# Backward sums of a two-layer GNN kernel: groups of four supertiles with shared node blocks

## The chip, the cores and the metric

The kernel runs on one core of a Trainium2 chip. A time is the device time of one execution in microseconds (us), and where several runs are told of, their median. Engines are named as in the profile: PE is TensorE's matmul, PEld its weight load, DVE is VectorE, ACT is ScalarE, POOL is GpSimd, SP is SyncE. Full speed of TensorE's clock is 2.4 GHz, its lower level is 1.2 GHz; the profile gives the granted clock as a share of full speed.

## What is computed

Two graph layers on 3125 nodes of 256 features and 100000 edges. The second one, whose backward half is changed here, is this (cut; `_typed_pass` is called once along the edges and once against them):

```python
def _typed_pass(feat, W, bias, src_idx, dst_idx, etypes, norm_per_edge, n):
    proj = jnp.einsum('ni,rio->rno', feat, W)          # 16 relations, 256 x 256 each
    m = proj[etypes, src_idx] + bias
    m = m * norm_per_edge[:, None]
    return segment_sum(m, dst_idx, num_segments=n)
norm_f = _inv_degree(dst, n)[dst]
m_forward = _typed_pass(feat, Wf, forward_bias, src, dst, etypes, norm_f, n)
norm_b = _inv_degree(src, n)[src]
m_backward = _typed_pass(feat, Wb, backward_bias, dst, src, etypes, norm_b, n)
s = feat @ loop_weight
return s + s + self_bias + m_forward + m_backward
```

The backward pass takes for each edge the row `proj[type, dst]` and adds it to the sum of node `src`; the sum is divided by the node's degree at the end.

## The kernel before

Edges are handled in 196 supertiles of 512 edges (128 partitions x `J` = 4). The nodes are 25 blocks of 128. `acc` in SBUF holds for each block 256 sums and, in two more columns (`AW` = 258), the degree.

The kernel has three long stages on the same engines: the first layer's messages, the forward sums (beside which the backward projections are computed and written to `proj[1]`), and last the backward sums, which alone are changed. Before the last stage the edges have been sorted by source node, not exactly: each supertile holds sources out of a few neighbouring blocks. `windows(1)` works out for each supertile the lowest block `lo`, the highest `hi` and a running count, and packs them in one word of `win[1]`; every engine reads these words with `windows_of`, a load followed by register arithmetic.

In the backward stage each engine runs its own loop, and semaphores alone order them:

- **POOL** (`sixes`, L431 to L442 by the profile's lines) gathers: for supertile `s` four indirect DMAs of 128 rows of 1 KB from `proj[1]` to slot `s % 12` of `raw2` (`RS` = 12). From supertile 12 on it waits before each supertile until `s_agg[2]` says that the supertile ten before it has been multiplied.
- **ACT** (`next_rows2`) copies the row numbers of later gathers into `gslot2`, two supertiles at a time.
- **DVE** (`compare2`, `add2`, driven by `backward`) makes one-hot keys of 128 x 1024 for each supertile (`match_nodes` at L1023: two blocks wide, for `lo` and `lo + 1`), in a ring of six (`HS`), four supertiles ahead; and adds the product, 2 x 258 columns in PSUM, to `acc` (L1081). If the supertile reaches beyond `lo + 1`, each further block is a round trip: keys of 128 x 512, a product in the PSUM bank `further_sums`, an addition (L1089).
- **PE** (`sum_backward`) waits for the keys, the gathered rows and the addition three supertiles back, then makes 8 f32 products of 128 x 258 (L745), 4 for each of two blocks, into one of three pairs of PSUM banks (`pair_sums`: `pu`, `pg`, `pa`). A further block is 4 more into `pc`, each after waiting for DVE. An f32 product stands in the profile as two LDWEIGHTS and two MATMUL, so that a supertile is 16 MATMUL there.

The bookkeeping of one supertile on PE and the waits in front of it are these lines:

```python
pe.wait_ge(s_oh[2], s + 1)
pe.wait_ge(s_gath[2][n], 16 * J * (rnd + 1))
if past(s, 3):
    pe.wait_ge(s_add[2], s - 2)
```

At the end `backward_mean` divides, and SP stores the result.

Of the kernel before, what the change touches and what calls it, by code (L numbers as in the profile page):

```python
# [4 lines left out]
F32 = mybir.dt.float32  # L5
F32R = mybir.dt.float32r
I32 = mybir.dt.int32
ALU = mybir.AluOpType
# [4 lines left out]
P = 128  # L13
# [5 lines left out]
J = 4  # L19
# [21 lines left out]
GS = 4  # L41
QS = 24
RS = 12
HS = 6
# [3 lines left out]
assert (ST - GS) % RS == 0  # L48


def gnn_program(nc, x, dst_l, src_l, typ_l, ea_t, W1, b1, W2, b2, Wg, bg, gamma, beta,
# [9 lines left out]
    with ctx:  # L61
# [88 lines left out]
        onehot2 = [fa[:, c:c + 2 * SE].rearrange("p (j n) -> p j n", j=J) for c in (8192, 9216, 4224, 5248, 2064, 3096)]  # L150
        further_onehot = fa[:, 6272:6272 + SE].rearrange("p (j n) -> p j n", j=J)
        PARTS = ((1, 0), (0, 1), (0, 0))

        pu = pb("pu", [P, HK, SE])
        pg = pb("pg", [P, J, H])
        pc = pb("pc", [P, J, H])
        pa = pb("pa", [P, 2, SE])
# [3 lines left out]
        pair_sums = [pu[:, :, :], pg[:, :, :].rearrange("p (a j) f -> p a (j f)", a=2), pa[:, :, :]]  # L161
# [140 lines left out]
        def sixes(eng):  # L302

            for s in range(RS + GS):
                yield s, s % RS, s // RS
            with eng.Fori(1, (ST - GS) // RS) as i:
                for m in range(RS):
                    yield RS * i + GS + m, (GS + m) % RS, i + (GS + m) // RS
# [80 lines left out]
        def _(pool):  # L389
# [226 lines left out]
        def _(pe):  # L616
# [122 lines left out]
            def sum_backward(s, n, rnd, w):  # L739

                lo, hi, wx = w

                def products2(out, keys):
                    for j in range(J):
                        last = nc.tensor.matmul(out[:, 0:AW], keys[:, j, :], raw2[:, n, j, :], start=(j == 0), stop=(j == J - 1))  # L745
# [9 lines left out]
                with pe.If(hi > lo + 1):  # L755
                    with pe.Fori(lo + 2, hi + 1) as b:
                        pe.wait_ge(s_xadd[2], wx + b)
                        pe.wait_ge(s_xoh[2], wx + b)
                        products2(further_sums, further_onehot).then_inc(s_xagg[2], 1)
# [81 lines left out]
            pe.wait_ge(s_add[1], ST)  # L841
            pe.wait_ge(s_win[1], 1)
            pe.wait_ge(s_ones, 1)
            for n, w in enumerate(windows_of(pe, 1, 0, GS)):
                sum_backward(n, n, 0, w)
            with pe.Fori(0, (ST - GS) // RS) as i:
                for m, w in enumerate(windows_of(pe, 1, RS * i + GS, RS)):
                    sum_backward(RS * i + GS + m, (GS + m) % RS, i + (GS + m) // RS, w)
# [3 lines left out]
        def _(dve):  # L852
# [45 lines left out]
            def windows(k):  # L898
# [3 lines left out]
                if k == 1:  # L902
                    link(nc.vector.tensor_scalar(first_neg, first_neg, float(2 - NB), None, ALU.max))
                    link(nc.vector.tensor_scalar(extra, first_neg, -1.0, 1.0, ALU.mult, ALU.add))
                    link(nc.vector.tensor_tensor(last, last, extra, ALU.max))
                link(nc.vector.scalar_tensor_tensor(out=extra, in0=last, scalar=float(-k), in1=first_neg, op0=ALU.add, op1=ALU.add))
                link(nc.vector.tensor_tensor_scan(count, extra, extra, float(NB), ALU.add, ALU.bypass))
                link(nc.vector.tensor_tensor(count, count, extra, ALU.subtract))
                link(nc.vector.scalar_tensor_tensor(out=count, in0=count, scalar=float(-k), in1=first_neg, op0=ALU.add, op1=ALU.add))
# [155 lines left out]
            def compare2(s, n, w):  # L1065

                lo, hi, wx = w
                if past(s, HS):
                    dve.wait_ge(s_agg[2], s - HS + 1)
                match_nodes(onehot2[n], iota_p, lo, s, src_f).then_inc(s_oh[2], 1)  # L1070

            def add2(s, n, w):

                lo, hi, wx = w
                first = dve.snap(nc.s_assert_within(lo, 0, NB - 2, skip_runtime_bounds_check_because="the windows are kept two blocks wide"))
                dve.wait_ge(s_xadd[2], wx + lo + 2)
                if past(s, 1):
                    dve.wait_ge(s_add[2], s)
                dve.wait_ge(s_agg[2], s + 1)
                t = acc[:, bass.ds(first, 2), :]  # L1080
                nc.vector.tensor_tensor(t, t, pair_sums[n % 3][:, :, 0:AW], ALU.add).then_inc(s_add[2], 1)  # L1081
                with dve.If(hi > lo + 1):
                    with dve.Fori(lo + 2, hi + 1) as b:
# [280 lines left out]
            for n, w2 in enumerate(windows_of(dve, 1, 0, 2)):  # L1364
                compare2(n, n, w2)
# [74 lines left out]
```

## Time and profile before

| | us |
|---|---|
| median of 3 runs | 4423.52 (4414.99 to 4432.65) |
| the profiled execution, own time | 4418.46 |
| its span, first to last instruction | 4416.7 |
| first to last gather issued in the backward stage | 3183.6 to 4367.5 |
| PE's first and last backward product | 3208.0 to 4397.9 |
| PE, DVE, POOL busy over the whole span | 79%, 56%, 52% |
| mean granted TensorE clock | 0.891 |

Matmuls are pipelined: two that follow each other start 0.22 us apart at full clock, while each is shown as 0.38 us long. So in the rows below 16 matmuls without a gap are shown as 3.65 us, and the next 16 begin 3.49 us after the first did. A number in square brackets in a timeline is the time that the engine had been idle, and what ended it; "issue" is a wait that the profile can't explain by a semaphore, "remote" one whose end the profile puts down to no engine or queue that it knows of.

### The profile page before, as it was taken

How to read it: one execution, taken by the hardware profiler on the slowest of the kernel's cores; microseconds unless marked ns; L12 is line 12 of the kernel's file. 1: busy time of each engine (PE TensorE's matmuls, PEld its weight loads, DVE VectorE, ACT ScalarE, POOL GpSimd, SP SyncE). 2: the span in 40 equal slices, each digit the busy share in tenths (PEclk: the TensorE clock that was granted, in tenths of full speed). 3: DMA queues.
4: the chain of work that ended last, by engine and by line, in shares of the span. 5: the costliest groups of instructions: out<-in, count | busy, mean ns of one | idle time of the engine just before them, and what ended most of it. 6: DMA issues, size and time to landing. Idle time of an engine off the chain costs nothing.

```text
span 4416.7 us, 72963 instructions
## 1 busy us (share of the span) xinstructions
PE 3478.9 (79%) x21136; PEld 2939.8 (67%) x21137; DVE 2476.3 (56%) x3465; ACT 1007.0 (23%) x1734; POOL 2308.7 (52%) x2362
## 2 busy tenths in 40 slices
PE   6999999999999979976666676767657766777776
PEld 5888888888888858864554555555445555665555
DVE  6888887888788888854554532222323333333334
ACT  3444444444444444410110110010100000000000
POOL 1555555555555500036555666656566655666663
PEclk8999999999999989988888888888867878888878
DMA  4555555555555525544443464444333322233332
GB/s 165 157 159 155 157 156 152 157 155 159 149 152 154 157 81 205 204 131 124 132 129 118 132 141 134 126 129 132 111 92 87 89 82 80 85 89 88 90 88 79
DMA packets 322746, 569.91 MB, mean 129 GB/s; under 512 B 73897, under 2 KB 218393, under 8 KB 322585
## 3 DMA queue, kind: packets, MB, share of 16 engines
q0 software_dynamic: 137984, 411.19, 33.2%
q1 hardware_dynamic: 182732, 154.33, 10.6%
q10 hardware_dynamic: 1868, 2.52, 0.2%
q8 instruction: 67, 1.10, 0.1%
q14 instruction: 95, 0.77, 0.1%
HBM read 452.43 MB, written 115.41 MB: 129 GB/s over the span
## 4 chain that ended last, share of the span: by engine, by line
PE 52%; issue 17%; DVE 12%; another core or an unknown queue 12%; DVEq 6%; ACT 1%; ACTq 0%; DMA 0%; POOL 0%; SPq 0%; POOLq 0%
PE pc L697 13%; PE pa L706 11%; PE pu L687 4%; PE pu L745 4%; PE pg L671 4%; PE pa L745 4%; PE pg L745 4%; DVE key L1249 3%; DVE tops L1246 3%; PE pu L679 3%; DVEq L277 1%; PE pu L800 1%; PE pc L659 1%; DVE onehot L1023 1%
## 5 line engine op out<-in xcount | busy, mean ns | idle before, releaser
L428 POOL DMA_INDIRECT fa<-proj,gslot x784 | 744.8, 950 | 865.6 <-issue 569.8
L416 POOL DMA_INDIRECT fa<-ptab,slot x784 | 814.2, 1039 | 721.8 <-issue 375.1
L440 POOL DMA_INDIRECT hr<-proj,gslot x784 | 745.8, 951 | 446.7 <-issue 226.3
L706 PE MATMUL pa<-fa,onehot 128*128 128x258 f32 x1760 | 517.1, 446 | 363.0 <-DVE onehot L1023 196.5
L706 PEld LDWEIGHTS pa<-fa,onehot 128*128 128x128 f32 x1760 | 379.7, 222 | 480.1 <-issue 374.8
L697 PE MATMUL pc<-ws,hr 128*128 128x256 f32 x4704 | 649.2, 290 | 43.2 <-issue 40.5
L697 PEld LDWEIGHTS pc<-ws,hr 128*128 128x128 f32 x4704 | 598.3, 193 | 64.5 <-issue 61.7
L745 PE MATMUL pu<-hr,fa 128*128 128x258 f32 x1056 | 295.6, 425 | 132.6 <-issue 129.2
L1056 DVE TENSOR_TENSOR acc<-acc,pa 128x258 f32 x196 | 82.7, 422 | 503.4 <-remote 303.8
L745 PEld LDWEIGHTS pu<-hr,fa 128*128 128x128 f32 x1056 | 225.2, 214 | 194.2 <-issue 157.5
L745 PE MATMUL pg<-hr,fa 128*128 128x258 f32 x1040 | 278.8, 417 | 74.5 <-issue 72.0
L1023 DVE SCALAR_TENSOR_TENSOR fa<-pc,base,src_f 128x1024 f32<-128x1024 f32 (+1 forms) x210 | 261.5, 1247 | 123.7 <-issue 109.3
L745 PE MATMUL pa<-hr,fa 128*128 128x258 f32 x1040 | 272.3, 408 | 67.2 <-issue 65.6
L503 ACT ACTIVATE hr<-pu 128x512 fp32r<-128x512 f32 x392 | 213.0, 596 | 459.5 <-remote 249.9
L745 PEld LDWEIGHTS pg<-hr,fa 128*128 128x128 f32 x1040 | 218.2, 211 | 129.0 <-issue 84.8
L1007 DVE SCALAR_TENSOR_TENSOR hr<-pu,hr 128x1024 fp32r<-128x1024 f32 x196 | 239.5, 1222 | 103.7 <-ACT hr L503 99.5
L745 PEld LDWEIGHTS pa<-hr,fa 128*128 128x128 f32 x1040 | 211.6, 204 | 115.3 <-issue 80.0
L514 ACT CAST hr<-fa 128x1024 fp32r<-128x1024 f32 x196 | 206.1, 1052 | 336.7 <-DVE fa L1030 293.6
L706 PE MATMUL pa<-hr 128*128 128x256 f32 x1760 | 251.4, 285 | 19.0 <-issue 13.8
L593 ACT COPY gslot<-row_dst 128x8 int32 (+1 forms) x98 | 18.8, 197 | 1083.9 <-DMA hr<-proj,gslot 1083.9
L1030 DVE TENSOR_TENSOR fa<-fa,pc 128x1024 f32<-128x1024 f32 x196 | 238.0, 1214 | 47.9 <-PE pc L697 29.5
L800 PE MATMUL pu<-hr 128*128 128x512 f32 x960 | 255.2, 409 | 8.5 <-issue 7.0
(153 smaller groups left out, 5048.8 us busy)
## 6 DMA issues: line engine op xcount, KB each, us to landing
proj<-fa SPq DMA_DIRECT2D x400, 256.0 KB
fa<-in_ea_t SPq DMA_DIRECT2D x196, 128.0 KB
fa<-ptab,slot POOLq DMA_INDIRECT x784
fa<-proj,gslot POOLq DMA_INDIRECT x784
hr<-proj,gslot POOLq DMA_INDIRECT x784
fa<-in_Wrel SPq DMA_DIRECT2D x32, 256.0 KB
ptab<-fa SPq DMA_DIRECT2D x25, 256.0 KB, 2.0
out<-res SPq DMA_DIRECT2D x4, 768.0 KB
```

Source lines behind the costliest of these rows:

```text
L416: pool.indirect_dma_start(pbuf[:, n % 2, j, :], None, ptab[:, :], bass.IndirectOffsetOnAxis(ap=slot[:, n, j:j + 1], axis=0)).then_inc(s_ga ...
L428: pool.indirect_dma_start(gbuf[:, n, j, 0:H], None, proj[0][:, :], bass.IndirectOffsetOnAxis(ap=gslot[:, at, j:j + 1], axis=0)).then_inc(s ...
L440: pool.indirect_dma_start(raw2[:, n, j, 0:H], None, proj[1][:, :], bass.IndirectOffsetOnAxis(ap=gslot2[:, n, j:j + 1], axis=0)).then_inc(s ...
L503: last = nc.scalar.activation(uT[:, par, 0, h, :, :].rearrange("p k e -> p (k e)"), pu[:, h, :], ACT.Relu)
L514: nc.scalar.copy(msg[:, par, 0, :, :], gate[:, par, :, :]).then_inc(s_mhi, 1)
L697: last = nc.tensor.matmul(pc[:, j, :], uT[:, par, a, j // 2, kk, j % 2 * P:(j % 2 + 1) * P], w2s[:, c, kk, :], start=False, stop=(j == jj ...
L706: last = nc.tensor.matmul(pa[:, bank, 0:width], keys[:, at, j, :], rows[:, j, :], start=(n == 0), stop=(n == len(todo) - 1))
L745: last = nc.tensor.matmul(out[:, 0:AW], keys[:, j, :], raw2[:, n, j, :], start=(j == 0), stop=(j == J - 1))
L800: last = nc.tensor.matmul(pslots[n], hT[:, a, kk, b * P:(b + 1) * P], wsp[:, u, c, kk, :], start=(not d and m == 0 and kk == 0), stop=(m = ...
L1007: nc.vector.scalar_tensor_tensor(out=uT[:, par, 1, :, :, :].rearrange("p h k e -> p h (k e)"), in0=pu[:, :, :], scalar=0.0, in1=uT[:, par, ...
L1023: return nc.vector.scalar_tensor_tensor(out=out, in0=numbers.unsqueeze(1).to_broadcast([P, J, width]), scalar=base[:, bass.ds(b, 1)], in1= ...
L1030: nc.vector.tensor_tensor(gate[:, par, :, :], gate[:, par, :, :], pc[:, :, :], ALU.mult).then_inc(s_msg, 1)
```

## The change

The unit of the backward sums becomes a group of four supertiles (49 groups) in place of one supertile.

- All PSUM banks become one tensor `banks`; the backward sums use two sets of three banks (`quad_sums`). The four supertiles of a group share a window of three blocks (`UB`), `lo` to `lo + 2`, where `lo` is the lowest of the group. The first two blocks are multiplied for every supertile, the third only for those that reach it (`third2` holds its keys in memory that is free by then). Since the third bank may get no product at all, a matmul of zeros opens it and another closes it in every group.
- All products of a group add up in PSUM; `s_agg[2]`, the addition on DVE (128 x 774) and `s_add[2]` come once per group.
- Blocks beyond the third are a round trip for the whole group.
- The ring of gathered rows has 16 slots in place of 12, the ring of keys 8 in place of 6. POOL waits once per group, for the group four before it, and DVE makes the keys of a group after the addition of the group two before it.
- `windows(1)` works out the windows of groups. The first group's keys are all made ahead of the last forward addition.

The core of the diff:

```diff
-RS = 12
-HS = 6
+RS = 16
+HS = 8
+UB = 3
...
-        pair_sums = [pu[:, :, :], pg[:, :, :].rearrange("p (a j) f -> p a (j f)", a=2), pa[:, :, :]]
+        quad_sums = [banks[:, 0:UB, :], banks[:, UB:2 * UB, :]]
...
-            for s, n, rnd in sixes(pool):
-                if past(s, RS):
-                    pool.wait_ge(s_agg[2], s - RS + 2)
+            for s, n, rnd, q in sixteens(pool):
+                if q >= RS // GS if isinstance(q, int) else n % GS == 0:
+                    pool.wait_ge(s_agg[2], q - RS // GS + 1)
...
-                pe.wait_ge(s_oh[2], s + 1)
-                pe.wait_ge(s_gath[2][n], 16 * J * (rnd + 1))
-                if past(s, 3):
-                    pe.wait_ge(s_add[2], s - 2)
-                for c in range(2):
-                    last = products2(pair_sums[n % 3][:, c, :], onehot2[n % HS][:, :, c * P:(c + 1) * P])
+                if past(q, 2):
+                    pe.wait_ge(s_add[2], q - 1)
+                nc.tensor.matmul(sums[:, 2, 0:AW], zeros[:, 0:P], zeros, start=True, stop=False)
+                lo, wx, most = w[0][0], w[0][2], bounded(pe, w[1][2])
+                for m in range(GS):
+                    n, at = n0 + m, (n0 + m) % HS
+                    pe.wait_ge(s_oh[2], GS * q + m + 1)
+                    pe.wait_ge(s_gath[2][n], 16 * J * (rnd + 1))
+                    if m == GS - 1:
+                        with pe.If(most > lo + 2):
...
+                    with pe.If(w[m][1] > lo + 1):
+                        products2(sums[:, 2, :], third2[at], n, stop=False)
+                    if m == GS - 1:
+                        nc.tensor.matmul(sums[:, 2, 0:AW], zeros[:, 0:P], zeros, start=False, stop=True)
+                    for c in range(2):
+                        last = products2(sums[:, c, :], onehot2[at][:, :, c * P:(c + 1) * P], n, start=(m == 0), stop=(m == GS - 1))
                 last.then_inc(s_agg[2], 1)
...
+            def compare_quad(q, at, w):
+                lo = w[0][0]
+                for n in range(GS):
+                    with dve.If(w[n][1] > lo + 1):
+                        match_nodes(third2[at + n], iota_p[:, 0:P], bounded(dve, lo + 2), GS * q + n, src_f)
+                    match_nodes(onehot2[at + n], iota_p, lo, GS * q + n, src_f).then_inc(s_oh[2], 1)
...
+            def add2(q, at):
+
+                lo, hi, wx = windows_of(dve, 1, GS * q, 1)[0]
...
+                dve.wait_ge(s_agg[2], q + 1)
+                t = acc[:, bass.ds(first, UB), :]
+                nc.vector.tensor_tensor(t, t, quad_sums[at // GS][:, :, 0:AW], ALU.add).then_inc(s_add[2], 1)
...
+            further_quad(0, windows_of(dve, 1, 0, 2))
+            next_quad(1, GS)
+            with dve.Fori(0, ST // GS // 2 - 1) as i:
+                for u in range(2):
+                    add2(2 * i + u, GS * u)
+                    next_quad(2 * i + 2 + u, GS * u)
```

How PE's instructions stand in the backward loop, before: one supertile (8 products into `pu`, then the jump over the further block, whose loop and products into `pc` stand behind it).

```order
L749 ISA
L745 MATMUL pu<-hr,fa 128x258 x8
L755 REGISTER_ALU x4
L755 COMPARE_AND_BRANCH
L756 ISA
L756 UNCONDITIONAL_BRANCH
L756 ISA
L757 REGISTER_ALU x2
L745 MATMUL pc<-hr,fa 128x258 x4
L756 ISA
L756 COMPARE_AND_BRANCH
L755 UNCONDITIONAL_BRANCH
```

After: the start of a group. L754 is the matmul of zeros, L768 guards the third block, whose keys are in `onehot` here.

```order
L281 TENSOR_LOAD win
L753 REGISTER_ALU
L754 MATMUL banks<-fa 128x258
L758 ISA
L759 ISA
L768 REGISTER_ALU x4
L768 COMPARE_AND_BRANCH
L749 MATMUL banks<-hr,onehot 128x258 x4
L768 UNCONDITIONAL_BRANCH
L749 MATMUL banks<-hr,fa 128x258 x8
```

The 8 products of a supertile stay as they were. The load of the windows comes once per group instead of once per twelve supertiles, the guarded products now stand ahead of a supertile's own and don't wait for DVE a second time, and the zero matmul is new.

DVE in the backward loop, before: the keys of one supertile (L1023), then the addition of one (L1081), in turn.

```order
L1023 REGISTER_ALU
L1023 ISA
L1023 SCALAR_TENSOR_TENSOR fa<-pc,base,src_f 128x1024
L1076 REGISTER_ALU x3
L1076 ISA
L1081 ISA
L1081 TENSOR_TENSOR acc<-acc,pg 128x516
L1082 REGISTER_ALU x3
L1082 COMPARE_AND_BRANCH
```

After: the addition of a group (L1129), and behind it the keys of the group two ahead, shown up to the first supertile's third block.

```order
L281 TENSOR_LOAD win
L1129 REGISTER_ALU
L1129 ISA
L1129 TENSOR_TENSOR acc<-acc,banks 128x774
L281 ISA
L281 TENSOR_LOAD win
L1099 REGISTER_ALU x4
L1099 COMPARE_AND_BRANCH
L1054 ISA
L1054 SCALAR_TENSOR_TENSOR onehot<-banks,base,src_f 128x512
L1099 UNCONDITIONAL_BRANCH
L1054 ISA
```

Four key instructions now follow one addition, and all four stand behind the wait for the group two before.

## Rows read from the trace of the kernel before

**Rows 1.** Windows, L440: stretch, POOL busy (gathers), granted clock, DMA share, GB/s.
```profile
3422.10:3869.20 447.10, 272.29 (x289) 0.82 0.29 84
3869.20:4345.10 475.90, 302.49 (x321) 0.83 0.31 88
3279.10:4345.10 1066.00, 665.52 (x705) 0.82 0.30 87
...
4174.40:4198.10 23.70, 15.12 (x16) 0.79 0.30 89
```
**Rows 2.** Timeline around two pauses of POOL: start, duration, engine, line, idle before.
```profile
4169.63 0.95 POOL L440 DMA_INDIRECT hr<-proj,gslot  x1 [0.30 <-issue]
4174.48 0.94 POOL L440 DMA_INDIRECT hr<-proj,gslot  x1 [3.90 <-remote]
...
4183.63 3.65 PE L745 MATMUL pg<-hr,fa 128*128 128x258 f32 x16
...
4187.12 0.82 PE L745 MATMUL pa<-hr,fa 128*128 128x258 f32 x3
...
4192.99 0.59 PE L745 MATMUL pa<-hr,fa 128*128 128x258 f32 x1 [2.22 <-issue]
...
4197.25 3.76 PE L745 MATMUL pa<-hr,fa 128*128 128x258 f32 x9 [0.81 <-issue]
4197.47 0.69 DVE L1081 TENSOR_TENSOR acc<-acc,pu 128x516 f32 x1 [10.20 <-remote]
4198.16 0.94 POOL L440 DMA_INDIRECT hr<-proj,gslot  x1 [3.99 <-remote]
```
**Rows 3.** Windows, L745: stretch, PE busy (matmuls), PEld busy (loads), clock, DMA, GB/s.
```profile
4174.40:4187.90 13.50, 13.50 (x58) 11.22 (x56) 0.92 0.33 95
4187.90:4197.20 9.30, 2.40 (x5) 1.04 (x4) 0.62 0.29 87
4197.20:4211.40 14.20, 14.15 (x57) 11.80 (x57) 0.89 0.31 88
```
**Rows 4.** Waits from 3183 to 4417: who waited for whom, us, times, longest.
```profile
DVE acc L1081 <- remote: 513.9, 64, 27.6
...
POOL hr L440 <- remote: 168.2, 52, 7.4
...
PE pc L745 <- DVE fa L1023: 82.4, 14, 16.0
```
**Rows 5.** Line L1023, 3255 to 4345: duration in ns, min/median/max; DVEq is DVE's sequencer.
```profile
L1023 DVEq FUSED_REGOPS  x196: 3/99/1394, 3255.7 to 4342.7; - x196
```
**Rows 6.** Start of the stage: POOL's first pauses in the timeline; PE's windows on L745.
```profile
3247.09 0.95 POOL L440 DMA_INDIRECT hr<-proj,gslot  x1 [0.30 <-issue]
3255.39 0.94 POOL L440 DMA_INDIRECT hr<-proj,gslot  x1 [7.35 <-remote]
...
3279.14 0.95 POOL L440 DMA_INDIRECT hr<-proj,gslot  x1 [4.06 <-remote]
...
3208.00:3222.00 14.00, 13.29 (x46) 10.68 (x46) 0.79 0.36 105
3222.00:3253.00 31.00, 6.27 (x11) 3.35 (x12) 0.54 0.32 93
```
**Rows 7.** Tile pc from 3180 on: count, ns min/median/max, first and last start.
```profile
L745 PE MATMUL pc<-hr,fa x112: 378/636/772, 3485.5 to 4139.0; 128*128 128x258 f32 x112
```
**Rows 8.** Groups by form, 3550 to 4417: busy us, mean ns of one, idle before.
```profile
L1023 DVE SCALAR_TENSOR_TENSOR fa<-pc,base,src_f 128x1024 f32<-128x1024 f32 x141 | 180.8, 1282 | 84.8 <-issue 76.5 <-PE pg L745 4.7 <-PE pa L745 2.9
L1081 DVE TENSOR_TENSOR acc<-acc,pg 128x516 f32 x48 | 33.0, 687 | 120.1 <-remote 104.1 <-PE pg L745 9.8 <-PE pa L745 3.5
L1023 DVE SCALAR_TENSOR_TENSOR fa<-pc,base,src_f 128x512 f32<-128x512 f32 x11 | 8.2, 750 | 7.0 <-issue 7.0
L1089 DVE TENSOR_TENSOR acc<-acc,pc 128x258 f32 x12 | 5.1, 424 | 43.9 <-PE pc L745 26.9 <-remote 12.3 <-issue 4.7
```
**Rows 9.** Timeline of the stage's end.
```profile
4367.49 0.94 POOL L440 DMA_INDIRECT hr<-proj,gslot  x1 [0.30 <-issue]
...
4370.22 3.65 PE L745 MATMUL pa<-hr,fa 128*128 128x258 f32 x16
...
4394.63 3.65 PE L745 MATMUL pu<-hr,fa 128*128 128x258 f32 x16
...
4398.52 0.69 DVE L1081 TENSOR_TENSOR acc<-acc,pu 128x516 f32 x1 [2.80 <-PE pu L745]
```
**Rows 10.** DMA queues, whole span (page) and 3320 to 4360: packets, MB, share of 16 engines.
```profile
q8 instruction: 67, 1.10, 0.1%
...
q0 software_dynamic: 32944, 89.98, 30.0%
```

More of the change, by code:

```diff
@@ L737, in sum_projections, with sum_backward, products2 @@
                 sum_further(k, n % 2, [gbuf[:, n, :, :]], AW, w)
-            def sum_backward(s, n, rnd, w):
-                lo, hi, wx = w
-                def products2(out, keys):
+            def sum_backward(q, n0, rnd, w):
+                sums = quad_sums[n0 // GS % 2]
+                def products2(out, keys, n, start=False, stop=True):
                     for j in range(J):
-                        last = nc.tensor.matmul(out[:, 0:AW], keys[:, j, :], raw2[:, n, j, :], start=(j == 0), stop=(j == J - 1))
+                        last = nc.tensor.matmul(out[:, 0:AW], keys[:, j, :], raw2[:, n, j, :], start=(start and j == 0), stop=(stop and j == J - 1))
@@ L902, in windows @@
                 if k == 1:
[L903 to L907, printed above, removed]
@@ L908, in windows @@
-                link(nc.vector.tensor_tensor(count, count, extra, ALU.subtract))
-                link(nc.vector.scalar_tensor_tensor(out=count, in0=count, scalar=float(-k), in1=first_neg, op0=ALU.add, op1=ALU.add))
+                    quads_of = lambda t: t.rearrange("p (q n) -> p q n", n=GS)
+                    least, most, more, total = (extra[:, n * ST // GS:(n + 1) * ST // GS] for n in range(4))
+                    nc.vector.tensor_reduce(least, quads_of(first_neg), AX.X, ALU.max)
+                    link(nc.vector.tensor_reduce(most, quads_of(last), AX.X, ALU.max))
@@ L1063, in add_sums, with further_quad @@
                 dve.sem_inc(s_done, 1)
[L1065 to L1083, printed above, removed]
+            def compare_quad(q, at, w):
[4 more added lines that the diff above has]
+                    match_nodes(onehot2[at + n], iota_p, lo, GS * q + n, src_f).then_inc(s_oh[2], 1)
+            def further_quad(q, w):
+                lo, wx, most = w[0][0], w[0][2], bounded(dve, w[1][2])
+                with dve.If(most > lo + 2):
+                    with dve.Fori(lo + 3, most + 1) as b:
                         dve.wait_ge(s_xadd[2], wx + b)
-                        match_nodes(further_onehot, iota_p[:, 0:P], b, s, src_f).then_inc(s_xoh[2], 1)
-                        dve.wait_ge(s_add[2], s + 1)
+                        for n in range(GS):
+                            last = match_nodes(further_onehot[n], iota_p[:, 0:P], b, GS * q + n, src_f)
+                        last.then_inc(s_xoh[2], 1)
                         dve.wait_ge(s_xagg[2], wx + b)
@@ L1089, in add2, with next_quad @@
                         nc.vector.tensor_tensor(t, t, further_sums[:, 0:AW], ALU.add).then_inc(s_xadd[2], 1)
+                        dve.wait_ge(s_xadd[2], wx + b + 1)
+            def next_quad(q, at):
+                w = windows_of(dve, 1, GS * q, GS)
+                compare_quad(q, at, w)
+                further_quad(q, w)
+            def add2(q, at):
+                lo, hi, wx = windows_of(dve, 1, GS * q, 1)[0]
+                first = dve.snap(nc.s_assert_within(lo, 0, NB - UB, skip_runtime_bounds_check_because="the windows are kept three blocks wide"))
+                if past(q, 1):
+                    dve.wait_ge(s_add[2], q)
+                dve.wait_ge(s_agg[2], q + 1)
+                t = acc[:, bass.ds(first, UB), :]
+                nc.vector.tensor_tensor(t, t, quad_sums[at // GS][:, :, 0:AW], ALU.add).then_inc(s_add[2], 1)
             def add_first(s, par, w):
```

88 lines of the change are left out of this document (50 added, 38 removed).

## The prediction, made blind

> **What bounds the kernel now.** Only the last 1.2 ms can change, so I read that stage alone: first the windows of POOL's gathers, then the timeline around its pauses, then PE's windows, last who waited for whom. The stage ends when PE has multiplied the last supertile; some 20 us of division and store follow and stay. Its pace is very even. Supertiles 16 to 191 take 1066.0 us (705 gathers in the window, of which 704 are these), 24.2 us for four; in the later half 475.9 us for 80, 23.8 us for four [rows 1].
>
> No engine is full. Four supertiles are 16 gathers, which POOL issues 1.25 us apart: 19.7 us. Then it pauses for 4.0 us, and the next 16 begin 23.7 us after the first 16 did [rows 1, 2]. PE has 64 matmuls for four supertiles, 14.0 us at full clock (16 take 3.49 us). But it does not do them evenly: 58 in the first 13.5 us, 5 in the next 9.3 us, and 57 in the 14.2 us after that [rows 3]. In that slow stretch PE is idle before single matmuls of one supertile, where there is no semaphore to wait for, at 2.2 and 0.8 us each, "issue"; DVE's sequencer needs up to 1.39 us for a register operation that mostly takes 0.10 [rows 2, 5]; and an addition whose product PE had finished by 4187.3 starts only at 4197.47, "remote", as POOL's pause ends at 4198.16 [rows 2]. In sum DVE waits 513.9 us and POOL 168.2 us for "remote" [rows 4]. So something that comes with unbroken gathering slows PE's and DVE's sequencers and the semaphores between the engines, from some 10 to 14 us after a burst of gathers begins until some 3 us after it ends. At the start of the stage the same is larger: 48 gathers without a pause, and in the last 31 us of them PE does 11 matmuls, half clock included [rows 6]. I can't name the mechanism, but its shape is clear: **POOL's unbroken gathering is what stops PE, and POOL stops only when the ring is full.** PE's capacity in one such cycle is some 64 to 67 matmuls, just what four supertiles need.
>
> **The change, part by part.** Against the profiled execution (4418.5 us, 5 us under the median):
>
> (a) *Ring of 16.* The first burst grows from 48 gathers to 64, which is 16 x 1.25 = 20 us more of crawling. Then POOL waits for a whole group of PE's (68 matmuls and its third blocks), where it waited for two supertiles. Before, supertile 16 is gathered from 3279.1 on [rows 6]. After: first gather at 3183.6 as before, 64 gathers end by about 3268, slow stretch over by 3274 (it outlasted the first burst by 5 us). DVE makes 4 keys instead of 2 and some third blocks ahead of the last forward addition, 2 x 1.28 + 4 x 0.75 = 5.6 us [rows 8], so PE starts near 3214. It does some 25 matmuls at speed and 22 in the crawl (11 in 31 us), and the rest of the first group, some 50, at 0.22 to 0.43 us: 11 to 21 us, done near 3290. **+11 us**, bounds +5 and +20.
>
> (b) *Blocks beyond two.* They are 112 matmuls in 14 round trips [rows 7], where PE waited 82.4 us for DVE, 16.0 at most [rows 4]. I followed the kernel's sorting on the reference's edges: it gives these 14, and after the change 29 supertiles that reach a third block and no group that reaches a fourth. So all round trips go. What that is worth shows in the pace: 24.2 us for four supertiles against 23.7 in the regular cycle, over the 44 groups from supertile 16 on 1066.0 - 44 x 23.7 = **-23 us**; the waits were mostly time in which the cycle would have stood anyway.
>
> (c) *Third blocks.* 29 supertiles x 8 matmuls, of which 23 lie in those 44 groups (groups 10 to 36, 13 of them). One costs 8 x 0.22 = 1.75 us at full and 3.4 at half clock. Since PE's capacity per cycle is just used up, and POOL now waits for the end of the group, they come after the slow stretch and lengthen the pause: 23 x 2.0 = **+46 us**, bounds 0 (they fit in a slow stretch) and 78.
>
> (d) *Matmuls of zeros.* Two products, 4 matmuls of 258 columns, 0.9 us for each group: 64 become 68, and 44 x 0.9 = 39 us if all are on the path. Up to 67 matmuls fit into a cycle by the rows above, so I take **+9 us**, bounds 0 and 39.
>
> (e) *Hand-overs.* Additions on DVE: 196 of 0.69 us become 49 of about 0.95 (258 columns take 0.42, 516 take 0.69 [rows 8]), some 90 us of DVE's busy time, all of it beside PE. Key instructions stay at 1.28 us. DVE's sequencer has, counted in the order of instructions, some 95 operations for four supertiles before and some 65 after, PE's about the same. **0**: DVE makes the keys of a group behind the addition of the group two before, 1 + 1 + 4 x 1.28 = 7 to 10 us with loads, while PE is in the group between, 15 us or more. Its cover is gone when the slow stretch catches the last keys; that is a rival below. PE's and DVE's increments fall by 147 each. The Trainium skill, "TensorE: Matmul & The Clock Gate", section on the per-tile semaphore tail, says that increments serialize, at 26 ns each; by it the 147 of PE are worth 4 us and the sum would be 4 us lower. The trace has no row for that; what it shows of semaphores is the 10.20 us wait above.
>
> (f) *The end.* Before, PE ends at 4398.3 (4394.63 and 3.65) [rows 9], 53 us after the gathers of supertile 192 begin (4345.1). After, when the last group's gathers have ended (19.7 us) and the slow stretch is over (3 us), PE has three groups of 68 matmuls left, 14.8 us each at the pace of [rows 9], 45 with some at half clock: 68 us. **+15 us**, bounds +8 and +18.
>
> Sum: 11 - 23 + 46 + 9 + 0 + 15 = **+58 us**. From the median of 4423.5: 4481.5, say 4482. Bounds added up: 5 - 23 + 0 + 0 + 8 = -10 and 20 - 23 + 78 + 39 + 18 = +132. For the likeliest case by itself 4440 to 4550.
>
> **Rivals.**
> 1. *The extra matmuls are absorbed.* PE enters a cycle a little further on, the zeros and two thirds of the third blocks fall into the slow stretch, and the pause stays at 4 us, set by the delivery of the semaphore. For it: "PE finished, semaphore late" is what [rows 2] show, and the pauses are equal to 0.1 us. Sum 11 - 23 + 15 + 0 + 12 = +15: 4438, no change. Chance 0.18.
> 2. *Fewer hand-overs shorten the slow stretch.* If sequencer operations and increments share what the gathers crowd, a third fewer on DVE could let PE finish a group inside the burst, and the pause falls from 4.0 to 2.5: 44 x 1.5 = 66 us less, third blocks at 20: 11 - 23 - 66 + 20 + 13 = -45: 4378. Against it: the gathers keep their 1.25 us throughout and are by far the most of the traffic. Chance 0.15.
> 3. *POOL becomes the bound.* No pauses: 196 x 5.0 = 980 us from 3184 to 4168, the last group 15 us later, against 4398.3: about 215 us less, 4208. It decides if PE's 73 matmuls a group (16 us) go on beside gathering. The first burst [rows 6] speaks against it. Chance 0.08.
> 4. *DVE becomes late.* Four keys stand in a row after one wait, some 30 sequencer operations; if half fall where one takes 0.7 us or more, the last keys come after the slow stretch, and PE waits 2.5 us in each group: 44 x 2.5 = 110 on top, 4592. It decides where a fourth key comes later than 10.5 us (three supertiles) into PE's group. Chance 0.06.
> 5. *The loops are loaded anew in each round.* PE's loop grows to sixteen supertiles with third and further blocks, some 1,350 instructions. In the stage before no instruction packet is seen between 3320 and 4360, though the whole run has 67 of 16 KB on one queue [rows 10]. Their share (0.1% of 16 engines over 4416.7 us) makes one about 1.1 us; six in each of twelve rounds, all on the path, are +79: 4561. The Trainium skill, "Runtime: NRT & Kernel Launch", section Instruction fetch mechanics, says that a taken branch out of the resident instructions forces a load, and gives PE 2048 instructions; by that figure the loop would still fit and this rival costs nothing. Chance 0.03.
>
> **How the numbers follow.** The forecast has 0.50. A measurement of this kernel can tell 0.5% (22 us) from no change, so faster is below 4401, slower above 4446. Rivals 2 and 3 are faster; rival 1 and the low end of the forecast are the same; the rest is slower: 0.23, 0.18, 0.59. The range leaves out rival 3 and part of 2 below, rivals 4 and 5 above: 4350 to 4550, some 0.8 inside.
>
> **What would show it.** Right: POOL's bursts of 16 with pauses of 4 to 5 us, longer (6 to 10) in the middle of the stage; PE idle at "issue" within groups; first pause of POOL after 64 gathers, near 3268, lasting some 20 us; no wait of PE for keys above some us; last gather near 4400. Wrong in the base: pauses clearly under 4 us, or a slow stretch that begins later than 14 us into a burst (rivals 2, 3); third blocks without longer pauses (rival 1); PE waiting for DVE at the third or fourth supertile of a group (rival 4); instruction packets within the stage (rival 5).

## The result, and the profile of the changed kernel

The changed kernel takes 4461.14 us (median; 4459.14 to 4463.66), the kernel before 4420.71 us in the same measurement: ratio 1.0088, 95% interval 1.0065 to 1.0111. It is slower by 0.9%, some 40 us; 4482 was forecast. The profiled run took 4459.21 us, with a span of 4457.4 us and a mean granted clock of 0.896, so its trace can stand beside that of [rows 1 to 9].

One thing has to be said first, because half of the experiments can't be read without it: the kernel before takes 4414 to 4421 us on the chip of this measurement and on one of the chips used below, and 3765 us on three others; every comparison below is between kernels that ran on one chip, and says on which kind.

POOL's windows on its gathers (columns: stretch, POOL busy with the number of gathers, granted clock, DMA share, GB/s), changed kernel; they answer to [rows 1]. The stretches are supertiles 16 to 191, the first 64 gathers, and the time from supertile 192's first gather to PE's end:

```profile
3289.10:4371.10 1082.00, 665.49 (x704) 0.85 0.30 85
3186.40:3271.40 85.00, 65.78 (x64) 0.60 0.34 98
4371.10:4438.80 67.70, 15.12 (x16) 0.95 0.11 31
```

POOL's timeline in the changed kernel (start, duration, engine, line, operation, idle before it in brackets): the first pause of the stage, two regular ones, one behind a group with four third blocks, and the last four of the stage:

```profile
3270.43 0.95 POOL L444 DMA_INDIRECT hr<-proj,gslot  x1 [0.30 <-issue]
3289.12 0.94 POOL L444 DMA_INDIRECT hr<-proj,gslot  x1 [17.74 <-PE banks L749]
...
3863.32 0.94 POOL L444 DMA_INDIRECT hr<-proj,gslot  x1 [11.87 <-PE banks L749]
...
4295.29 0.94 POOL L444 DMA_INDIRECT hr<-proj,gslot  x1 [3.99 <-remote]
...
4318.93 0.94 POOL L444 DMA_INDIRECT hr<-proj,gslot  x1 [3.94 <-remote]
...
4341.09 0.94 POOL L444 DMA_INDIRECT hr<-proj,gslot  x1 [2.46 <-remote]
...
4371.14 0.94 POOL L444 DMA_INDIRECT hr<-proj,gslot  x1 [10.36 <-PE banks L749]
```

The bursts of 16 gathers are still 19.7 us long, and the regular pause is still 4.0 us (4295.29 to 4318.93 is 23.64 us, where it was 23.7 [rows 1, 2]). PE's windows on L749 (PE busy with matmuls, PEld busy with loads, clock, DMA, GB/s), once for the two parts of a regular cycle and once for the cycle with four third blocks, answer to [rows 3]:

```profile
4105.20:4118.70 13.50, 12.96 (x54) 10.77 (x53) 0.91 0.33 97
4118.70:4128.00 9.30, 3.97 (x13) 2.24 (x12) 0.83 0.30 85
...
3831.80:3845.30 13.50, 13.50 (x63) 11.73 (x62) 1.00 0.34 97
3845.30:3854.40 9.10, 4.25 (x9) 1.75 (x8) 0.67 0.30 86
3854.40:3863.30 8.90, 8.05 (x28) 6.29 (x28) 0.77 0.00 0
```

The slow stretch is still there: 54 matmuls in 13.5 us, then 13 in 9.3 us. In the cycle with third blocks 28 matmuls are left when the burst is over; POOL waits for all of them, and nothing moves meanwhile (DMA 0.00).

In most other cycles POOL doesn't wait for PE's work. These are the last 16 matmuls of a group with one third block (76 matmuls), and the gather that waited for that group:

```profile
4162.43 3.65 PE L749 MATMUL banks<-hr,fa 128*128 128x258 f32 x16
...
4176.34 0.94 POOL L444 DMA_INDIRECT hr<-proj,gslot  x1 [4.09 <-remote]
```

PE had ended the group at 4166.1, 6 us before the burst of gathers ended; POOL went on 10 us after PE's end, 4 us after its own burst. So the pause of 4 us is the time until PE's increment is seen, and a group can grow by some microseconds before the pause does. Who waited for whom from 3186 to 4457 answers to [rows 4] (us, times, longest):

```profile
DVE acc L1129 <- remote: 614.2, 35, 18.3
...
POOL hr L444 <- remote: 135.3, 34, 4.2
POOL hr L444 <- PE banks L749: 94.0, 11, 17.7
```

No row says that PE waits for DVE: the 82.4 us for `pc` in [rows 4] are gone. The additions are 49 in place of 196:

```profile
L1129 DVE TENSOR_TENSOR acc<-acc,banks 128x774 f32 x49 | 47.1, 961 | 918.1 <-remote 614.2
```

**Where the 40 us are.** The two profiled runs, by the start of supertile 0's, 16's and 192's first gather and PE's end:

| stretch | before | changed | difference |
|---|---|---|---|
| up to the first gather of the stage | 3183.6 | 3186.4 | +2.8 |
| to supertile 16's first gather | 95.5 | 102.7 | +7.2 |
| supertiles 16 to 191, 44 groups | 1065.9 | 1082.0 | +16.1 |
| to PE's end | 53.2 | 67.6 | +14.4 |

The last 18.4 to 18.6 us are the same in both.

### The profile page after: what moved, and what is told of

It is laid out like the page before. It is cut to its first block, busy times and chain, and to the rows that moved or that the text cites. A ratio compares the mean times of both kernels' runs of the same rounds, so it can differ in the third digit from the quotient of the medians.

```text
span 4457.4 us, 71978 instructions
## 1 busy us (share of the span) xinstructions
PE 3564.8 (80%) x21452; PEld 2996.2 (67%) x21453; DVE 2391.6 (54%) x3325; ACT 1007.0 (23%) x1734; POOL 2297.9 (52%) x2362
## 4 chain that ended last, share of the span: by engine, by line
PE 60%; issue 16%; DVE 12%; another core or an unknown queue 7%; DVEq 4%; ACT 1%; ACTq 0%; DMA 0%; POOL 0%; POOLq 0%
PE banks L749 20%; PE banks L701 12%; PE banks L710 11%; PE banks L691 4%; PE banks L675 4%; DVE key L1289 4%; DVE tops L1286 3%; PE banks L683 3%; PE banks L815 2%; DVEq L281 1%; DVE onehot L1054 1%; PE banks L663 1%; PE banks L636 1%; DVEq L1082 1%
## 5 line engine op out<-in xcount | busy, mean ns | idle before, releaser
L749 PE MATMUL banks<-hr,fa 128*128 128x258 f32 x3136 | 847.3, 419 | 217.1 <-issue 214.0
L749 PEld LDWEIGHTS banks<-hr,fa 128*128 128x128 f32 x3136 | 654.8, 210 | 393.5 <-issue 290.5
L710 PE MATMUL banks<-fa,onehot 128*128 128x258 f32 x1760 | 518.5, 447 | 361.6 <-DVE onehot L1054 232.7
L710 PEld LDWEIGHTS banks<-fa,onehot 128*128 128x128 f32 x1760 | 381.2, 222 | 475.4 <-issue 364.8
L701 PE MATMUL banks<-ws,hr 128*128 128x256 f32 x4704 | 642.2, 289 | 49.6 <-issue 47.0
L701 PEld LDWEIGHTS banks<-ws,hr 128*128 128x128 f32 x4704 | 590.6, 193 | 72.0 <-issue 69.7
L815 PE MATMUL banks<-hr 128*128 128x512 f32 x2400 | 608.0, 402 | 15.8 <-issue 14.3
L815 PEld LDWEIGHTS banks<-hr 128*128 128x128 f32 x2400 | 471.0, 197 | 122.7 <-issue 17.0
L1129 DVE TENSOR_TENSOR acc<-acc,banks 128x774 f32 x49 | 47.1, 961 | 918.1 <-remote 614.2
L710 PE MATMUL banks<-hr 128*128 128x256 f32 x1760 | 252.6, 285 | 21.5 <-issue 15.9
L597 ACT COPY gslot<-row_dst 128x8 int32 (+1 forms) x98 | 18.6, 197 | 1069.8 <-DMA hr<-proj,gslot 1069.8
L1067 DVE TENSOR_TENSOR hr<-fa,hr 128x1024 fp32r<-128x1024 f32 x196 | 240.6, 1228 | 23.5 <-ACT hr L518 5.2
```

The lines of the kernel that those rows point to most:

```text
L701: last = nc.tensor.matmul(pc[:, j, :], uT[:, par, a, j // 2, kk, j % 2 * P:(j % 2 + 1) * P], w2s[:, c, kk, :], start=False, stop=(j == jj ...
L710: last = nc.tensor.matmul(pa[:, bank, 0:width], keys[:, at, j, :], rows[:, j, :], start=(n == 0), stop=(n == len(todo) - 1))
L815: last = nc.tensor.matmul(pslots[n], hT[:, a, kk, b * P:(b + 1) * P], wsp[:, u, c, kk, :], start=(not d and m == 0 and kk == 0), stop=(m = ...
L1067: nc.vector.tensor_tensor(msg[:, par, 1, :, :], gate[:, par, :, :], msg[:, par, 0, :, :], ALU.subtract).then_inc(s_mlo, 1)
```

## The experiments

Two explanations stand against each other. **Theory A**: POOL still slows PE by its unbroken gathering, the cycle of 23.7 us stands as before, and what is lost is the extra work that comes after the slow stretch, third blocks above all. **Rival B**: the ring of sixteen and the wait for a whole group are the loss, because POOL's bursts and pauses get longer whatever PE computes. A third, that nothing but PE's matmul work sets the pace, is asked by taking gathers away.

**e5 and e6: both kernels again, unedited.**

> The changed kernel unchanged, beside the kernel before on the same chip. The runs so far show two conditions: the kernel before takes 4420 us with slow stretches of PE and DVE while POOL gathers, and 3765 us without any. Theory (the change costs only where the slow stretches make POOL wait for whole groups): with slow stretches 1.009 of before again; without them POOL's 784 gathers of 1.25 us set the stage in both kernels, and the change costs the work behind the last gather and the later start alone, 0.999 to 1.003. Rival (the matmuls of zeros and third blocks cost everywhere): 1.01 or more in both conditions.

> The kernel before, unchanged, for its trace in this condition. Theory: either bursts of 16 gathers with pauses of 4 us and PE at a crawl (4420 us), or no pause at all after the first wait and 1.25 us for each of 784 gathers (3765 us). Rival: pauses of another size, from a ring that is full for another reason.

Measured, on a chip where the kernel before takes 4414.31 us: changed kernel 4464.12 us (4457.53 to 4476.03), ratio 1.0119 [1.0088, 1.015]; the profiled execution of the kernel before, 4414.78. POOL's windows of supertiles 16 to 191, changed and before:

```profile
3297.80:4376.80 1079.00, 665.34 (x704) 0.85 0.30 86
```
```profile
3279.60:4340.00 1060.40, 665.33 (x704) 0.83 0.30 87
```

From the first gather to supertile 16's it is 102.8 against 95.4 us, in the middle 1079.1 against 1060.4, at the end 66.5 against 54.6: +7.4, +18.7, +11.9. So the three differences within the stage come again. What differs from pair to pair is when the stage begins: 10.8 us later here, 2.8 in the first. Nothing in the stages ahead is meant to change, and I have no cause for it.

**e7: third blocks' products left out.** DVE still writes their keys, and the zeros stay; PE leaves 29 x 8 matmuls out, and with them the guard (L768: register operations and a branch) that stands ahead of each of the 196 supertiles.

```diff
-                    with pe.If(w[m][1] > lo + 1):
-                        products2(sums[:, 2, :], third2[at], n, stop=False)
```

> The changed kernel without PE's products of third blocks (29 supertiles' share of a third block is left out of the sums; DVE still makes the keys, the matmuls of zeros stay). Theory: with slow stretches the long pauses of 7 us go and 26 to 35 us with them, ratio to before about 1.002; without slow stretches PE has room beside POOL, nothing changes (within 3 us of the changed kernel). Rival (the zeros and the group wait are the cost, not the third blocks): with slow stretches 1.007 or more remains.

Measured beside e5 and e6: 4454.01 us (4452.65 to 4470.56), ratio 1.0104 [1.0073, 1.0135]. That is 10 us less than e5, and the intervals overlap: the expectation of 1.002 failed, and the rival's mark, 1.007 or more, was met. The trace shows why. From the first gather to supertile 16's it is 95.2 us, 7.6 less than e5 and just what the kernel before needs, so the third blocks, with their guards, were the whole loss there: POOL's first pause waits for group 0 alone, which has four of them. In the middle the pauses of 5 to 12 us behind third blocks are gone too, but it still takes 1083.0 us, because something else comes six times: two bursts with no pause, or one of under 2.5 us, between them, and a long pause behind. POOL's timeline, then PE's windows over the same stretch:

```profile
3406.41 0.94 POOL L444 DMA_INDIRECT hr<-proj,gslot  x1 [3.94 <-remote]
...
3426.42 0.94 POOL L444 DMA_INDIRECT hr<-proj,gslot  x1 [0.30 <-issue]
...
3460.24 0.94 POOL L444 DMA_INDIRECT hr<-proj,gslot  x1 [14.13 <-PE banks L749]
```
```profile
3406.40:3421.00 14.60, 14.06 (x62) 11.80 (x62) 0.96 0.33 97
3421.00:3446.00 25.00, 5.67 (x13) 2.86 (x11) 0.57 0.36 105
3446.00:3460.20 14.20, 9.76 (x30) 6.85 (x30) 0.67 0.04 12
```

PE's increment was seen before the burst was over and released four slots at once: POOL went on for 32 gathers. The slow stretch then lasts from 14.6 us after the burst's start to its end, 25 us with 13 matmuls, and POOL waits 14.13 us for what is left. Two groups take 53.8 us instead of 2 x 23.7 = 47.4. The six pairs (53.8, 54.7, 50.8, 53.7, 54.6, 55.1) cost 38 us together, more than the 27 us by which the groups with third blocks lengthen the same stretch in the changed kernel. Without them it would be 1083.0 - 38 = 1045 us, 15 us less than the kernel before needs (1060.4): so of the rival's two causes this points to the wait for groups, by way of these pairs, and not to the zeros. The same thing stands once in the changed kernel, at its end: pauses of 2.46 and 10.36 us, 22.2 and 30.0 us for two groups, +4.8 us; and once in e5 (2.50 and 10.63).

What lets an increment through early is not shown. Another of the six pairs, with PE's last matmuls of the group, DVE's addition, which waits for the same increment, and POOL's next gather:

```profile
4054.75 3.65 PE L749 MATMUL banks<-hr,fa 128*128 128x258 f32 x16
...
4064.12 0.96 DVE L1127 TENSOR_TENSOR acc<-acc,banks 128x774 f32 x1 [11.62 <-remote]
...
4067.74 0.94 POOL L444 DMA_INDIRECT hr<-proj,gslot  x1 [0.30 <-issue]
```

The burst began at 4047.1, so the group ended 11.3 us into it. The six groups that released such a burst ended 8.6 to 11.6 us into theirs; those behind a regular pause, 10.4 to 15.4. Being ahead goes with it, but the ranges overlap. Nor is it shown that the missing third blocks are the reason: three of the six pairs (at 3406, 4047 and 4220) stand among groups that have no third block in the changed kernel either, and what differs there in PE's own work is only the missing guard.

What follows: the slow stretch lasts on to the burst's end at least (25 us with 13 matmuls in a burst of 32 gathers, 9.3 us in one of 16), as theory A has it, but "fewer matmuls, less time" doesn't follow from it. **Here less work of PE came with more long bursts**, which took most of the gain. Rival B keeps a part: the wait per group is what makes such bursts a whole group longer. (That a finer wait would avoid them in this condition was asked by e9, e10 and e12, and stayed open.)

**e1 and e8: the changed kernel with a ring of eight.**

```diff
-RS = 16
+RS = 8
```

> The changed kernel with RS = 8 in place of 16: POOL fills two groups ahead instead of four. Theory (unbroken gathering slows PE, the cycle of 23.7 us for 16 gathers stands whatever the ring): first burst 32 gathers instead of 64, group 2 gathered from about 3250; the cycle unchanged; after the last gather one group is left to PE instead of three. Together some 25 us less than the changed kernel: 4430 to 4440, about 1.003 of before. Rival (a deep ring hides latency of the hand-over between POOL and PE): each of 46 groups costs 2 us more or worse, 4530 or above.

> The changed kernel with RS = 8, in whichever of the two conditions this chip is. With slow stretches, theory (terms of the start and the end): first burst 32 gathers instead of 64, one group left to PE after the last gather instead of three, the cycle of 23.7 us kept: 20 to 30 us less than the changed kernel, 1.004 to 1.006 of before. Rival (the deep ring carries PE over the slow stretches): 1.012 or more. Without slow stretches: 1.001, as before.

Both came on chips where the kernel before takes 3765 us. Measured: 3769.84 us, ratio 1.0011 [1.0001, 1.002], and 3770.2 us, ratio 1.0014 [1.0004, 1.0023]. POOL's windows of e1, supertiles 16 to 191 and those before; then its only pause:

```profile
2845.70:3728.00 882.30, 667.64 (x705) 0.99 0.36 105
2748.50:2845.70 97.20, 65.21 (x64) 0.82 0.30 86
```
```profile
2791.88 0.95 POOL L444 DMA_INDIRECT hr<-proj,gslot  x1 [0.30 <-issue]
2805.64 0.95 POOL L444 DMA_INDIRECT hr<-proj,gslot  x1 [12.81 <-PE banks L749]
```

There is no slow stretch and no second pause: 20.05 us for each group, which is 16 gathers at 1.25 us (a gather of 0.95 us and 0.30 us until the next). On such a chip this stage is what rival 3 of the prediction described, POOL the bound, whatever the ring. The one pause of 12.81 us, with all eight slots (32 gathers) filled before PE has finished its first group, is the price of waiting for groups with a ring of only two groups.

**e2: the kernel before with a ring of six.**

```diff
-RS = 12
+RS = 6
```

> The kernel before with RS = 6 in place of 12. Same theory: the pace of 23.7 us for four supertiles stands, first burst 24 gathers instead of 48, and 5 supertiles instead of 9 are left to PE after the last gather: 13 to 20 us less than before, about 4403. Rival (the ring hides latency): slower than before by 1% or more.

On the chip of e1: 3744.92 us, ratio 0.9942 [0.9925, 0.9958], the best time of all kernels here that compute the whole result, and below the kernel before by 20.6 us. POOL never pauses:

```profile
2821.80:3702.00 880.20, 665.70 (x704) 1.00 0.37 105
```

PE's waits for DVE at the round trips add up to 24.8 us (14 times), in place of 82.4 where the slow stretches are, and none shows in POOL's pace. I have no trace of the unedited kernel on such a chip, so which of its waits the smaller ring takes away isn't shown; nor was it run where the slow stretches are.

**e3 and e11: the changed kernel with one gather in four.** Three quarters of the rows are left out, and the waits of PE and ACT on the gathers are fitted to that (not shown); PE and DVE do all they did.

```diff
-                for j in range(J):
+                for j in range(1):
```

> The changed kernel with one of the four gathers of each supertile; the other three quarters of the rows are left out, and the sums are of what stood in the buffer. PE, DVE and their semaphores do the same work. Theory (gathering slows them): no slow stretch, PE sets the pace with 14.8 us for a group and 1.8 for a third block, the stage takes some 800 us, the kernel 4020 to 4060. Rival (PE's and DVE's own instruction stream or the clock makes the slow stretch): the cycle stays above 20 us, the kernel above 4250.

> The changed kernel with one of the four gathers of each supertile (three quarters of the rows left out). Where the kernel before takes 4420 us, theory (gathering makes the slow stretches): none is left, a group takes 14.8 us and 1.75 for each third block as where the kernel before takes 3765 us. Rival (the condition slows PE and DVE by themselves): matmul gaps of 2 us within groups remain, a group takes 18 us or more. Without slow stretches in before: 14.8 us again.

Measured, both times on the 3765 us kind of chip: 3574.39 and 3573.2 us. What was asked, whether the slow stretches go when the gathers go, could not be seen, since they aren't there with all gathers either. But the run measures PE's own pace. POOL's timeline at two group starts, PE's window between them, and POOL's waits:

```profile
3421.49 0.95 POOL L444 DMA_INDIRECT hr<-proj,gslot  x1 [10.11 <-PE banks L749]
...
3436.33 0.95 POOL L444 DMA_INDIRECT hr<-proj,gslot  x1 [10.13 <-PE banks L749]
```
```profile
3421.50:3436.30 14.80, 14.26 (x65) 12.10 (x65) 1.00 0.12 35
```
```profile
  PE banks L749: 519.1, 45
```

A group of 68 matmuls takes 14.84 us, 0.218 us each. With one third block it is 16.6, with two 18.3, three 20.1, four 21.8: **1.75 us per third block**, and the four matmuls of zeros are, by the same 0.218 us each, an estimated 0.87 us of the 14.84.

**e4: the changed kernel with gathers of 256 bytes per row.** All 784 gathers, a quarter of the bytes. By the edit the row numbers are as before while the table has four times as many rows, so other rows come, all out of its first quarter.

```diff
-                    pool.indirect_dma_start(raw2[:, n, j, 0:H], None, proj[1][:, :],
+                    pool.indirect_dma_start(raw2[:, n, j, 0:H // 4], None, proj[1].rearrange("r (k f) -> (r k) f", k=4),
```

> The changed kernel with all 784 gathers, each of 128 rows of 256 B instead of 1 KB (out of the same table; three quarters of each row are left out). Theory by count (number of gathers, descriptors and semaphore increments): cycle stays 23.7 us, kernel within 1% of 4461. Theory by bytes: the slow stretch goes or shortens, POOL's 20.0 us for a group becomes the bound, kernel about 4250.

Measured, on the chip of e1: 3750.39 us, 20.0 us per group, no pause. The gathers' line:

```profile
L444 POOL DMA_INDIRECT hr<-proj,gslot x784: 940/944/4840, 2738.5 to 3720.5; - x196
```

POOL needs 944 ns for a gather of 128 rows of 256 B, and 946 ns for one of a kilobyte a row (e12): where POOL is the bound the number of gathers counts, not their bytes. Whether the bytes or the issuing make the slow stretches remains open, for the same reason as in e3.

**e9, e10 and e12: ring of sixteen, but the increment after every supertile.** POOL waits for the one supertile whose slot it fills, DVE for four increments.

```diff
-                if q >= RS // GS if isinstance(q, int) else n % GS == 0:
-                    pool.wait_ge(s_agg[2], q - RS // GS + 1)
+                if past(s, RS):
+                    pool.wait_ge(s_agg[2], s - RS + 2)
...
-                last.then_inc(s_agg[2], 1)
+                    last.then_inc(s_agg[2], 1)
...
-                dve.wait_ge(s_agg[2], q + 1)
+                dve.wait_ge(s_agg[2], GS * q + GS)
```

> The changed kernel, but PE increments after every supertile again and POOL waits for supertiles (ten before the one it gathers have... s - 14 done) as in the kernel before, with 16 slots; sums and additions stay by group. With slow stretches, theory (POOL's wait for whole groups makes the pauses of 7 to 8 us after groups with third blocks, and bursts of 32 gathers where PE is ahead): neither occurs, 10 to 20 us less than the changed kernel, ratio to before 1.006 to 1.009, what is left being start and end. Rival (the group wait costs nothing, the extra matmuls do): no change, 1.010 to 1.013. Without slow stretches: within 0.2% of before.

> The changed kernel with a wait of POOL and an increment of PE for every supertile, ring of 16, in whichever condition this chip is. With slow stretches, theory: no pauses of 7 to 8 us in mid-stage and no burst of 32 gathers, 10 to 20 us less than the changed kernel, 1.006 to 1.009 of before. Rival (the group wait costs nothing): 1.010 to 1.013. Without slow stretches: 0.997 again.

> The changed kernel with its ring of sixteen, but PE's increment comes after every supertile again, POOL waits for the one supertile whose slot it fills, and DVE for four increments. Two things can be met here. Where the kernel before takes about 4415 us (slow stretches of PE while POOL gathers): theory A, a wait per group makes the state of affairs lumpy (a group that PE finishes inside a burst gives an unbroken 32 gathers, and that costs 6 to 7 us each): with a wait per supertile POOL's pauses come shorter and oftener, the long pauses behind groups with third blocks shrink, 4425 to 4445 us, ratio 1.003 to 1.007. Theory B, the size of the ring and the third blocks are the whole cost, whatever the unit of the wait: 4455 to 4470, ratio 1.010 to 1.012. Where the kernel before takes about 3765 us (no slow stretches): POOL alone sets the pace, 3755 to 3760 us, ratio 0.997 to 0.998, as in the two runs before.

All three came on the 3765 us kind: 3754.87, 3759.49 and 3755.35 us, ratios 0.9971 [0.9962, 0.9981], 0.998 [0.9971, 0.999] and 0.9975 [0.9966, 0.9985]. For this kind, e9's expectation (within 0.2% of before) was narrowly missed, the other two held. POOL's and PE's windows of e12:

```profile
2827.30:3707.40 880.10, 665.63 (x705) 0.99 0.36 105
```
```profile
3407.40:3427.40 20.00, 14.88 (x65) 11.89 (x64) 1.00 0.35 105
```

Here PE does a group in 14.9 of 20.0 us, and third blocks, zeros and hand-overs all fit into the 5 us that are left. So on such a chip the kernel with shared blocks, a ring of sixteen and the finer wait is 0.2 to 0.3% faster than the kernel before; what of that the shared blocks give isn't shown, and the kernel of e2, which has none, gains more. Compared with e8 on the same chip, e9 is 15.3 us faster; it has both a larger ring and the finer wait, so I can't divide the two, but the pause of 11.72 us that e8's trace shows, like the one in e1, is most of it. The unedited changed kernel wasn't run on such a chip, and the finer wait wasn't met with slow stretches.

## Why the prediction was right, term by term

The sign, the size (+58 forecast, +40 measured) and the shape held: bursts of 16 with pauses of 4 us, longer in the middle, a first pause of 17.74 us after 64 gathers at 3271.4 (forecast near 3268, some 20 us), and the last gather at 4389.9 (near 4400). By its steps:

- **(a) Start, +11.** Measured +10.0 to supertile 16, of which 2.8 lie ahead of the stage, so 7.2 (7.4 in the second pair). The path held: POOL waits for the whole first group, counted at some 97 matmuls and done near 3290 (100 and 3288.3 measured). But I charged the time to the longer crawl of a ring of sixteen and to DVE's keys; e7 has both and starts as fast as the kernel before (95.2 us against 95.5). What costs is the 32 matmuls of the four third blocks in group 0, 7.0 us at the 1.75 us of e3. That the whole +10 comes so near +11 is in part luck, because the 2.8 us ahead of the stage are in no term.
- **(b) Round trips, -23.** The cycle behind it held: 23.7 us stays the regular interval, and no interval has a wait for `pc` any more. Five intervals of 24.1 to 24.3 hold one gather that starts 0.64 us later than the others (0.94 us of "issue" before it in place of 0.30); it comes every 112 gathers, while POOL's loop turns every 64, and the kernel before has such gathers 144 apart. The cause is open.
- **(c) Third blocks, +46.** This is the term that was mis-sized. The middle is 1082.0 - 44 x 23.7 = 39.2 us above the regular cycle; 26.6 of it are the seven intervals behind groups with third blocks (those between 25.7 and 31.6 us), 3.7 the one at 3289 (27.4), 4.8 the long burst near the end, 2.5 the five late gathers, the rest the 0.05 us of each cycle. With 23 third blocks that is 1.2 us each where I took 2.0. The interval at 3289 waits for group 1 and its two third blocks, which the term left out; it is 23.8 in e7, so with it they are 30 us for 25. The step that failed is "PE's capacity per cycle is just used up": it isn't. The group of 76 matmuls shown above ended 10 us before POOL went on, and of the 13 groups with third blocks in the middle only seven are followed by a clearly longer interval. A block costs 1.75 us at full clock (e3), and what of it fits before the increment is seen is absorbed.
- **(d) Zeros, +9.** Nothing that can be seen: the regular interval is 23.7 to 23.8. They cost an estimated 0.87 us a group where PE sets the pace (e3); here the wait for the semaphore does, and they lie under it. Together (b), (c) and (d) were forecast at +32 and measured at +16.
- **(e) Hand-overs, 0.** DVE was never late; no row has PE waiting for it. The rule quoted from the Trainium skill, "TensorE: Matmul & The Clock Gate", on the per-tile semaphore tail, says that increments serialize at some 26 ns each; by that rule 147 fewer are an estimated 4 us, something like 0.1 us in each cycle, and the regular cycle doesn't show it (23.7 to 23.8 us, 23.7 before). A difference so small is not settled by these runs.
- **(f) End, +15.** Measured +14.4 (+11.9 in the second pair). Three groups end after the last gather, as forecast: the one under way, still slowed, at 4409.1, then two at some 14.9 us each; 48.9 us from 4389.9, where it was 30.8 before (4367.5 to 4398.3).

Of the rivals, 1 (absorbed) holds for the zeros and for about a third of the third blocks' time (1.2 us of 1.75). 2 (fewer hand-overs shorten the slow stretch) is not seen, the pause is 4.0 us with a quarter of the additions. 4 (DVE late) is not seen. 5 (loops loaded anew) is not: from 3375 to 4440 there is no instruction packet, and between 3320 and 4400 three of 16 KB on this queue and one of 8 KB on another, all before 3375:

```profile
q8 instruction: 3, 0.05, 0.0%
```

In the same place the Trainium skill, "Runtime: NRT & Kernel Launch", Instruction fetch mechanics, gives PE room for 2048 instructions; that a loop of some 1,350 is not fetched again after its first pass agrees with this row. 3 (POOL the bound) did not come in the forecast's condition, but is what all runs on the other kind of chip show. What the prediction did not see is the pair of bursts: an increment seen early costs 3 to 8 us (50.8 to 55.1 us for two groups in place of 47.4). It would not have moved the forecast much, since the changed kernel meets it once, but it makes the sum of such terms unsafe, as e7 showed.

Two slips in the prediction's working change nothing in the sum. Rival 3's 980 us from 3184 end at 4164, not 4168, and the chances for "slower" add the whole forecast, its low end included. (a) and (f) came near their size, 21.6 us of the 26 forecast; the three terms of the middle came to half of theirs, 16 of 32.

## What to carry to other kernels

Before shared work is priced, ask which resource the shared step uses and whether that one sets the pace; here the matmuls were free as long as the group ended well before its increment was seen, and cost time when it ended later (7.9 us for the four blocks behind the longest interval). Where a producer slows its own consumer while it runs, the size of each release sets the size of the bursts (16 gathers here, 32 when two came together), and taking work away may give little, as in e7. A smaller ring gained 20.6 us where there are no slow stretches (e2); where they are it wasn't tried. And read the same kernel on more than one chip before a mechanism of one trace is made the reason for a change.

## What the runs showed of the hardware

**The same kernel takes 4415 us on some chips and 3765 on others.** The granted clock over the span is 0.89 there and 0.975 here. The cycle with slow stretches is 23.7 us, without them 20.0; POOL's gather takes the same 0.95 us in both. In the fast kind PE, DVE and the semaphores go on beside gathering without slow stretches, with the DMA share even higher (0.36 against 0.30). The last stage alone isn't all of it: the stage begins at 2737 to 2749 us on the one kind and at 3184 to 3195 on the other, so the stages ahead, which gather as well, differ by some 445 us. Within a measurement the kernels stay in one kind. What makes a chip one or the other, and by which path the gathers reach the sequencers of the other engines, is open: every run made to ask it (e3, e4, e11) came on a chip without slow stretches. So that the gathers cause the slow stretches is read from their timing, in bursts of 16 and of 32, and not shown by a run without them.

**Byte count didn't matter for the issuing engine.** A gather of 128 rows occupies POOL for 0.94 to 0.95 us plus 0.30 at 1 KB (e12) or 256 B a row (e4); the smaller one lands after 2.4 us (median) in place of 2.7.
